# Attention's key loads in six halves at set phases, and the values stored by head group

## What is computed

```python
def heads(y):
    return y.reshape(B, L, H, HD).transpose(0, 2, 1, 3)
q = heads(x @ Wq + bq)
k = heads(x @ Wk + bk)
v = heads(x @ Wv + bv)
scores = jnp.einsum('bhqd,bhkd->bhqk', q, k) / np.sqrt(HD).astype(x.dtype)
attn = jax.nn.softmax(scores, axis=-1)
out = jnp.einsum('bhqk,bhkd->bhqd', attn, v)
```

## Time and profile before

| | us |
|---|---|
| median of 3 runs | 3345.98 (3341.54 to 3361.2) |
| profiled execution | 3342.29, its span 3341.0 |
| TensorE busy | 3222.9 (96% of the span) |
| VectorE busy | 2069.4 (62%) |
| ScalarE busy | 1395.4 (42%) |
| GpSimd busy | 1470.4 (44%) |
| queue of GpSimd's DMAs | 31.5% of 16 engines' span, 234.90 MB |
| queue of SP's DMAs | 23.1%, 228.54 MB |
| granted TensorE clock, mean | 0.978 |

### The profile page before, as it was taken

One profiled execution on the slowest core, in us unless ns is written; L12 is line 12 of the kernel. 1 busy time (PEld: TensorE's weight loads), 2 busy tenths in 40 slices (PEclk: granted clock), 3 DMA queues, 4 the chain that ended last, 5 costly groups with the idle time before them and its releaser, 6 DMA issues.

```text
span 3341.0 us, 44195 instructions
## 1 busy us (share of the span) xinstructions
PE 3222.9 (96%) x16794; PEld 2203.2 (66%) x16794; DVE 2069.4 (62%) x3524; ACT 1395.4 (42%) x2739; POOL 1470.4 (44%) x662
## 2 busy tenths in 40 slices
PE   8798999999999999999999986999999999999999
PEld 7686655555555555555555534788888888778888
DVE  4647778878788788778778744733333332236666
ACT  2121366666566666666666662311111111012332
POOL 0200478778677778778777674300000000002222
PEclk9899999999999999999999998999999999889999
DMA  5474488888879879888887667700111112201221
GB/s 193 138 222 142 144 207 184 194 201 186 193 175 203 203 174 211 187 194 202 187 191 183 164 147 229 252 13 26 38 38 38 38 38 78 76 28 65 73 73 52
DMA packets 186172, 466.26 MB, mean 140 GB/s; under 512 B 27077, under 2 KB 69309, under 8 KB 154216
## 3 DMA queue, kind: packets, MB, share of 16 engines
q0 software_dynamic: 32256, 234.90, 31.5%
q1 hardware_dynamic: 153703, 228.54, 23.1%
HBM read 151.94 MB, written 75.76 MB: 68 GB/s over the span
## 4 chain that ended last, share of the span: by engine, by line
PE 84%; DMA 8%; DVE 4%; issue 2%; ACT 1%; POOL 1%; SPq 0%; DVEq 0%; POOLq 0%; ACTq 0%
PE ps L359 13%; PE ps L621 12%; PE ps L633 12%; PE ps L1075 11%; PE ps L1064 11%; DMA accd<-pt 6%; PE ps L433 4%; PE ps L1595 3%; PE ps L639 3%; PE ps L1608 3%; PE ps L437 2%; PE ps L1628 2%; PE ps L937 1%; PE ps L1425 1%; ACT pt L689 1%
## 5 line engine op out<-in xcount | busy, mean ns | idle before, releaser
L372 DVE TENSOR_REDUCE nmp<-ps 128x1 f32<-128x512 f32 x1966 | 1201.7, 681 | 165.4 <-PE ps L359 164.3
L689 ACT ACTIVATE pt<-ps 128x512 f32<-128x512 f32 x2048 | 1033.1, 627 | 559.2 <-PE ps L621 559.0
L777 POOL TENSOR_TENSOR pacc<-pacc,pt 128x2048 f32<-128x2048 f32 x192 | 909.1, 4735 | 46.5 <-ACT pt L689 41.6
L621 PE MATMUL ps<-qs,ks 128*128 128x512 f32 x2048 | 821.2, 403 | 7.5 <-issue 5.3
L359 PE MATMUL ps<-ks,qs 96*128 96x512 f32 x1966 | 809.2, 412 | 8.6 <-DVE nmp L372 5.4
L359 PEld LDWEIGHTS ps<-ks,qs 96*128 96x128 f32 x1966 | 375.4, 191 | 277.8 <-DVE nmp L372 170.6
L633 PE MATMUL ps<-pt,vq 128*32 128x512 f32 x4096 | 494.9, 601 | 0.0
L621 PEld LDWEIGHTS ps<-qs,ks 128*128 128x128 f32 x2048 | 392.1, 192 | 107.8 <-ACT pt L689 24.9
L1064 PE MATMUL ps<-hpb,w 128*128 128x512 f32 x1536 | 381.9, 398 | 3.3 <-DMA x_d<-x 3.3
L1075 PE MATMUL ps<-w,gp 128*128 128x512 f32 x1536 | 380.5, 396 | 2.2 <-DVE gp L1208 2.2
L1075 PEld LDWEIGHTS ps<-w,gp 128*128 128x128 f32 x1536 | 289.4, 188 | 71.5 <-DVE gp L1208 2.7
(11 more groups left out here) (168 smaller groups left out, 3211.4 us busy)
## 6 DMA issues: line engine op xcount, KB each, us to landing
accd<-pt POOLq DMA_DIRECT2D x224, 1024.0 KB, 9.0
qk_d<-st SPq DMA_DIRECT2D x128, 256.0 KB, 2.7
ks<-qk_d SPq DMA_DIRECT2D x24, 1024.0 KB, 17.6
qs<-qk_d SPq DMA_DIRECT2D x96, 256.0 KB, 6.8
xina<-in_x SPq DMA_DIRECT2D x8, 1024.0 KB, 6.5
v_d<-vst SPq DMA_DIRECT2D x32, 256.0 KB, 2.4
vq<-v_d SPq DMA_DIRECT2D x8, 1024.0 KB, 13.9
recb<-r_d SPq DMA_DIRECT2D x32, 256.0 KB
```

The lines of the kernel that those rows point to most:

```text
L372: dve.tensor_reduce(nmp[:, n // 4, n % 4:n % 4 + 1], ps[:, ring.bank["max", u], :], AX.X, ALU.max, negate=True).then_inc(s_mr, 1)
L621: pe.matmul(ps[:, n % 3, :], ksb[w % 2][:, hh, 128 * kt:128 * kt + 128], qsb[:, v % 3, hh, :], start=True, stop=True).then_inc(s_sc, 1)
L689: act.activation(pt[:, g % 8, hh, :], ps[:, n % 3, :], ACT.Exp, scale=SCALE).then_inc(s_exp, 1)
L777: pool.tensor_tensor(pacc[:, :, :], first, pt[:, g % 8, :, :], ALU.add).then_inc(s_add, 1)
```

## The change

Each key piece is cut in two halves of two heads (0.5 MB). The six halves are issued in phases 1, 3 and 4 of the group's first unit and again of its second. Each waits for the scores up to its own phase (s_sc at 64 v + 8 f). The first group's pieces, in the first stage, are also halves, two after one another. v_d becomes [8, 128, 16, 128]: for each group and partition the 16 key tiles in a row, 8 KB contiguous. A store of values writes four runs of 512 bytes for each row where it wrote one of 2 KB; a load reads one run of 8 KB for each partition where it read 16 of 512 bytes. The load of values moves to phase 4 of the third unit.

```diff
@@ -148,7 +148,7 @@
 def program(nc, a):
     pe, act, dve, pool, sp = nc.tensor, nc.scalar, nc.vector, nc.gpsimd, nc.sync
     qk_d = nc.dram_tensor("qk_d", [B, 4, D, S], F32, kind="Internal").ap()
-    v_d = nc.dram_tensor("v_d", [B * S, D], F32, kind="Internal").ap()
+    v_d = nc.dram_tensor("v_d", [4 * B, 128, S // 128, 128], F32, kind="Internal").ap()
     ao_d = nc.dram_tensor("ao_d", [NT, 128, D], F32, kind="Internal").ap()
     r_d = nc.dram_tensor("r_d", [2, 4, CH], F32, kind="Internal").ap()
     x2_d = nc.dram_tensor("x2_d", [B * S, D], F32, kind="Internal").ap()
@@ -372,10 +372,11 @@
             dve.tensor_reduce(nmp[:, n // 4, n % 4:n % 4 + 1], ps[:, ring.bank["max", u], :], AX.X, ALU.max,
                               negate=True).then_inc(s_mr, 1)
 
-        def sp_load_k(w, r):
-            b, f, part = w // 4, 128 * (w % 4), (2, 3, 2)[r]
-            sp.dma_start(ksb[w % 2][32 * r:32 * r + 32, :, :].bitcast(F32),
-                         qk_d[b, part, f:f + 128, :].rearrange("(h e) s -> e h s", e=HD)).then_inc(s_kd[w % 2], 16)
+        def sp_load_k(w, r, half):
+
+            b, f, part = w // 4, 128 * (w % 4) + 64 * half, (2, 3, 2)[r]
+            sp.dma_start(ksb[w % 2][32 * r:32 * r + 32, 2 * half:2 * half + 2, :].bitcast(F32),
+                         qk_d[b, part, f:f + 64, :].rearrange("(h e) s -> e h s", e=HD)).then_inc(s_kd[w % 2], 16)
 
         def sp_load_q(v):
             w, qc = divmod(v, NCH)
@@ -573,7 +574,8 @@
                             sp.wait_ge(s_qst[r], 128)
                         sp.wait_ge(s_pad, 3)
                     if ci == NCH and j in (1, 3, 5):
-                        sp_load_k(0, j // 2)
+                        sp_load_k(0, j // 2, 0)
+                        sp_load_k(0, j // 2, 1)
                     if ci == NCH and j in (6, 7):
                         sp_load_q(j - 6)
                     if ci == NCH + 2 and j == 0:
@@ -592,9 +594,9 @@
                             sp.dma_start(qk_d[b, 2 * (j // 4) + x, 128 * (j % 4):128 * (j % 4) + 128,
                                               CH * c:CH * c + CH], st[:, r, :].bitcast(F32)).then_inc(s_qst[r], 16)
                     else:
-                        rows0 = CH * ci + 128 * (j - 8)
                         sp.wait_ge(s_vev, 4 * ci + j - 7)
-                        sp.dma_start(v_d[rows0:rows0 + 128, :], vst[:, j - 8, :]).then_inc(s_vst[j - 8], 16)
+                        sp.dma_start(v_d[4 * b:4 * b + 4, :, 4 * c + j - 8, :].rearrange("w p e -> p w e"),
+                                     vst[:, j - 8, :].rearrange("p (w e) -> p w e", w=4)).then_inc(s_vst[j - 8], 16)
@@ -613,7 +615,7 @@
             w, n = v // NCH, 4 * g + hh
             if kt == 0 and hh == 0:
                 pe.wait_ge(s_qd[v % 3], 48 * (v // 3 + 1))
-                pe.wait_ge(s_kd[w % 2], 48 * (w // 2 + 1))
+                pe.wait_ge(s_kd[w % 2], 96 * (w // 2 + 1))
                 pe.wait_ge(s_md, 32 * (v + 1))
                 pe.wait_ge(s_pad, 5 if w else 3)
             if n >= 3:
@@ -780,9 +782,7 @@
             pool_values(NU - 1)
 
         def sp_load_v(w):
-            b, f = w // 4, 128 * (w % 4)
-            sp.dma_start(vq[:, w % 2, :, :],
-                         v_d[S * b:S * b + S, f:f + 128].rearrange("(t p) e -> p t e", p=128)).then_inc(s_vq[w % 2], 16)
+            sp.dma_start(vq[:, w % 2, :, :], v_d[w]).then_inc(s_vq[w % 2], 16)
 
         def sp_fold_sums(v):
@@ -830,12 +830,13 @@
                     sp_row(v + 1)
                 if f == 7 and v:
                     sp_store_ao(v - 1)
-                if v + NCH - c < NU and (c, f) in ((0, 6), (1, 4), (1, 7)):
+                if v + NCH - c < NU and c < 2 and f in (1, 3, 4):
+                    i = 3 * c + (1, 3, 4).index(f)
                     sp.wait_ge(s_pad, 5)
-                    if w >= 2:
-                        sp.wait_ge(s_sc, 256 * (w - 1))
-                    sp_load_k(w, ((0, 6), (1, 4), (1, 7)).index((c, f)))
-                if v + NCH - c < NU and (c, f) == (2, 7):
+                    sp.wait_ge(s_sc, 64 * v + 8 * f)
+                    sp_load_k(w, i // 2, i % 2)
+                if v + NCH - c < NU and (c, f) == (2, 4):
+                    sp.wait_ge(s_sc, 64 * v + 8 * f)
                     if w >= 2:
                         sp.wait_ge(s_pv, 64 * (w - 1))
                     sp_load_v(w)
```

More of the change, by code:

```diff
@@ L296, in pe_early @@
                 pe.wait_ge(s_qd[v], 48)
-                pe.wait_ge(s_kd[0], 48)
+                pe.wait_ge(s_kd[0], 96)
             if u == 64:
```

## The result

The changed kernel takes 3396.91 us in the median of 4 runs (3394.74 to 3399.03), the kernel before 3344.86 us in four runs beside it. The ratio is 1.0156 (95% interval 1.0132 to 1.0180): 1.6% slower, where a small gain was forecast, and outside the range of 3313 to 3353. The profiled execution took 3397.03 us, its span 3395.7.

The account below looks back on a forecast made before the run. TensorE was 84% of the chain; its waits for accd in attention were the loss to remove. 27.1 - 11.7 - 2.8 - 0.8 = 11.8 us off 3342.3 gave 3330 us, range 3313 to 3353.

Parts of the forecast that it names:

- What bounds the kernel, and what the phase 7 piece cost: Attention stretch: key piece in second unit's phase 7 slows kt 12; TensorE waits 15.3 us for accd in third units.
- at most 27.1 us: Upper bound of the gain over 27 attention units: accd waits and clock losses go once the phase 7 piece goes.
- Phases 3 and 4 coincide behind recb, kt 8 is late, additions are just too late: First and second units: both halves leave together behind recb, kt 8 is late, TensorE waits for pacc, 0.6 us a unit.
- the sum: Net gain from all terms: 27.1 - 11.7 - 2.8 - 0.8 = 11.8 us.
- the slip: Last addition in first and second units comes 0 to 1.7 us later; taken as 0.3 in the mean, 13 units.
- recb ... comes 0 to 2.7 us later: SP's queue, first and second units: phase 1 half ahead of queries, r_d and recb delays recb by 0 to 2.7 us.
- Half the price of 1 MB beside one accumulation: Cost bound for the 0.5 MB of phase 1: 2.7 us, half of 5.4 us for 1 MB beside an accumulation.
- Near the lower end, since most of the piece's own packets are done before r_d is issued: Reason given for taking the last addition's delay as 0.3 us, within 0 to 1.7 us.
- The prediction's own sign of being wrong: GpSimd's aout more than 35 us after the copy of accv, against 33.4 in unit 5 before.
- The slower rival: Phase 1 half delays recb, aout, kt 12 and last addition: 3.3 us in each of 13 units, 3366 us; chance 0.10.
- The clock: TensorE's granted clock falls after its waits in attention; 2.7 us counted in two units, expected back with the gain.
- Values, stores, first keys, lateness of keys and queries: Smaller terms: values beside kt 8 cost 2.8 us, stores of v 0.8 us; first keys, key and query lateness nothing.

Follow-up runs that it names:

- keys in phase 0: Kernel before, with whole 1 MB key pieces moved to phase 0 of first, second and third units, after kt 12's transfer landed: 3313.37 us, ratio 0.9884.
- the layout run: Kernel before with only the new layout of the values, all places as before: 3351.40 us, ratio 1.0011; profiled execution 3364.7 us.
- the run with it alone: Changed kernel with only the half of phase 1 on ScalarE's queue, the halves of phases 3 and 4 left on SP's: 3337.17 us, ratio 0.9977.
- the first experiments: Four runs timed together: one half early alone 3366.57, recb first 3352.19, three halves behind recb 3397.54, values at old place 3405.27 us.

## Why the prediction was wrong

*What bounds the kernel, and what the phase 7 piece cost.* Right. All waits for accd went with that piece. The bound of "at most 27.1 us" comes from one execution: keys in phase 0 brought 36.7 us by the medians (24 to 54 by the interval of the ratio). In the profiled execution of the layout run, a long one, whose order of transfers is that of before, 26 intervals lost 1347.9 - 1296.6 = 51.3 us, and its waits were longer:

```profile
L695 ACT ACTIVATE accv<-ps x27: 597/597/598, 481.2 to 1829.1; 128x512 f32<-128x512 f32 x27
```

```profile
PE ps L639 <- DMA accd<-pt: 22.7, 7, 4.5
PE ps L639 <- POOL pacc L777: 9.9, 6, 2.8
```

*Phases 3 and 4 coincide behind recb, kt 8 is late, additions are just too late.* Right as a mechanism. The run in which ScalarE issues the early half, 4.8 us earlier, is the kernel that I had in mind: 3337 us, profiled 3330.2, and 12.0 us of waits for pacc in 10 waits, where the sum had 13 x 0.6 = 7.8 for this and 3.9 for the slip.

*"recb ... comes 0 to 2.7 us later", and a slip of the last addition of 0 to 1.7 us, of which I took 0.3.* This step failed. recb leaves 3.9 us later and not 0 to 2.7: r_d to recb grew from 7.1 to 11.0 us in the mean of the 13 units. Half the price of 1 MB beside one accumulation was taken for a delay that goes through two steps. The half was landed (at 605.4) before r_d was issued (607.73), as the prediction says, but it had made the three query loads late in their turn, the last of them 13.0 us after its issue, and kt 2 and kt 4 as well, and r_d went out among those. "Near the lower end, since most of the piece's own packets are done before r_d is issued" was therefore wrong in effect. Then recb itself, which the sum left at its old 11.6 us, took 13.5 in the mean to the start of aout (10.5 before, all 13 units): it left behind kt 8 in unit 4, where it had gone 2.5 us ahead of it in unit 5 before, and the pair left with it. Together aout starts 7.0 us later after the fold than before (35.3 and 28.2), and the last addition is 4.1 us too late in the mean and not 0.9. The prediction's own sign of being wrong, aout more than 35 us behind the copy of accv, came: 39.8. The slower rival named the place and the chain rightly and its size wrongly: 3.3 us a unit for 4.1 measured, and 3366 us.

*The clock.* It was counted only as part of the gain. The losses of the changed kernel are 90.2 us, the waits 56.0 + 4.6. The other 29.6 us go together with a lower granted clock around the waits. Over the 27 intervals, after and before (length, busy times of the engines, PEclk, DMA share, GB/s):

```profile
433.00:1869.70 1436.70, 1376.01 (x7807) 759.24 (x7803) 1096.39 (x1863) 887.87 (x1756) 1053.07 (x406) 0.98 0.82 184
433.40:1807.00 1373.60, 1354.43 (x7807) 755.22 (x7803) 1095.73 (x1863) 886.42 (x1755) 1047.79 (x405) 1.00 0.85 192
```

0.02 of 1436.7 us is some 29 us, though a part of the slow stretches lies in the waits themselves. Three stretches at the start of units 5 and 6:

```profile
650.00:660.00 10.00, 10.00 (x49) 4.55 (x42) 5.66 (x9) 4.12 (x8) 2.41 (x3) 0.77 0.51 147
660.00:670.00 10.00, 10.00 (x56) 6.31 (x59) 8.99 (x16) 7.75 (x16) 8.78 (x3) 1.00 1.04 251
700.00:710.00 10.00, 5.68 (x44) 1.37 (x40) 0.97 (x2) 1.08 (x2) 7.38 (x2) 0.79 0.42 87
```

0.77 and 0.79 of full, between the two levels of 1.2 and 2.4 GHz, while TensorE is busy for all of 10 us in the first; 1.00 again from 660. Over the fourteen waits of 4 us in the mean 29.6 us are 2.1 us each, an estimate that gives the clock all that the waits leave. In the slower rival this would have added 13 x 2.1 = 27 us, close to the 31 us by which it fell short.

*Values, stores, first keys, lateness of keys and queries.* The values had 2.8 us in the sum, the stores 0.8: neither shows in a run. No wait that the profile puts down to keys or queries came, as said. That the half delays queries without harm was right, and hid that it delays what follows them.

*The rule of the Trainium skill* (*DMA: Bandwidth & Descriptors*, Queues, rings and completion order: an engine takes turns between queue rows) was set aside for contention between queues. The same section of the Trainium skill has the descriptors of one ring taken up in ring order, by which r_d would stand behind what SP issued before it. No run here shows that apart from the time of the load, and kt 2 and kt 4 of unit 4, 12.1 us each for 10.1 and 9.8 in another queue, show that not all of the delay is of that kind.

## What to carry to other kernels

Before a bulk load is moved, list the small transfers that follow it and for which an engine waits, and follow each through its own chain; half a megabyte in a free-looking slot cost some 60 us here (3397 against 3337, with the pair in place), because an 8 KB transfer came behind it in thirteen units. Issue bulk loads when the DMA engines are idle, early enough to have landed before the small transfers go: from SP's own queue this made the kernel 1.2% faster than it was. A queue of its own for the bulk is not shown to help: where it went with a gain, the early half had also moved in time, and the pair on ScalarE's queue went once with a faster kernel (3325 against 3337 us) and once with a slower one (3410 against 3397). When a wait of several microseconds on TensorE is priced, count the slower clock with it.

## What I had not expected of the hardware

The same loads from ScalarE's queue, the early half 4.8 us earlier, were worth 72 us (3396.9 to 3324.8). The half took 4.3 us to land there in unit 4 (4.1 in the run with it alone), and 7.5 us in the changed kernel.

A load in another queue is not harmless: with the pair on ScalarE's queue, leaving together with recb, recb needed 16.7 us (615.34 to 632.07); with the pair 0.7 us behind it in its own queue 13.9.

1 MB of keys lands in 7.2 us in the median when the accumulations are quiet (keys in phase 0) and in 17.6 us, up to 21.2, in the kernel before.

The times of one kernel spread by 1% (before: 3326 to 3357 us beside the first experiments). The longer ones tend to have the lower granted clock (0.982 at 3334 us and 0.976 at 3358, both of the kernel before). In the layout run's long profiled execution, at the start of a third unit, a stretch with waits reads:

```profile
900.00:910.00 10.00, 6.94 (x24) 3.61 (x21) 3.63 (x6) 2.37 (x5) 0.61 (x1) 0.54 0.34 105
```

0.54 of full over 10 us. That the spread comes from such stretches was not tested.
